# Moving normalisations, value evictions and rotary additions between the engines of a pipelined decoder layer, with new instruction lists

## The reference, cut to what matters

```python
# 1: rotary self attention, 16 heads of 16
q = (ln(x) @ Wq + bq), kv = (ln(x) @ Wkv + bkv)
q, k = rotary(q * s, x), rotary(k * s, x)      # the rotation is scaled by |x| of the row
w = softmax(causal(ln_head(q) @ ln_head(k).T / 4))
x1 = ln(x + (w @ v) @ Wo + bo)
# 2: attention along the 256 features of x1, 8 heads of 8, band of 64
q, k, v = split(x1.T @ w_in.T + b_in)
o = softmax(band(q @ k.T / sqrt(8))) @ v @ w_out.T + b_out
x2 = ln(x1 + w_ct(relu(o) * ctx) + b_ct)
# 3: feed-forward with ternary weights
g, u = x2 @ wgu.T;  h = silu(g) * u;  h = h / rms(h)
out = ln(x2 + h @ w_proj.T)
```

## Time and profile before

| | |
|---|---|
| median of three executions | 1081.5 us (1079.98 to 1083.27) |
| profiled execution, its time | 1079.87 us |
| profiled execution, its span | 1078.1 us |
| busy share of the span | PE 87%, DVE 88%, ACT 68%, POOL 76% |
| granted PE clock, mean | 0.95 of 2.4 GHz |

### The profile page before, as it was taken

How to read it: one execution, slowest core, us unless ns; L and a number is a source line. 1 busy time by engine, 2 the same in 40 slices (tenths; PEclk the granted TensorE clock), 3 DMA queues, 4 the chain that set the end, 5 groups by cost and what they waited for, 6 DMA issues and landing times.

```text
span 1078.1 us, 26386 instructions
## 1 busy us (share of the span) xinstructions
PE 933.3 (87%) x10449; PEld 547.9 (51%) x10484; DVE 944.7 (88%) x1877; ACT 734.7 (68%) x1203; POOL 816.3 (76%) x1197
## 2 busy tenths in 40 slices
PE   3366688899999999999999999999999999889885
PEld 1133355455555555555555555555555555555453
DVE  3779878899999999999999999999999999988644
ACT  1344356677778777777777777777777777777754
POOL 2764468788988888888889888888888888854542
PEclk9677679899999999999999999999999999999979
DMA  7000000000000000000000000000000000000000
GB/s 230 0 21 6 12 17 17 17 17 12 22 22 23 22 12 23 23 22 22 22 15 19 23 22 22 14 21 22 23 22 22 17 17 17 18 17 17 18 5 20
DMA packets 26122, 25.06 MB, mean 23 GB/s; under 512 B 6160, under 2 KB 24976, under 8 KB 26000
## 3 DMA queue, kind: packets, MB, share of 16 engines
q1 hardware_dynamic: 24368, 20.23, 6.6%
q10 hardware_dynamic: 1632, 3.15, 0.9%
HBM read 14.19 MB, written 4.19 MB: 17 GB/s over the span
## 4 chain that ended last, share of the span: by engine, by line
DVE 47%; PE 24%; ACT 12%; POOL 8%; issue 7%; DMA 1%; SPq 1%; POOLq 0%; DVEq 0%
DVE rowmax L1265 12%; POOL prob L1013 5%; DVE hsplit L1322 4%; ACT kT L758 4%; PE ps L420 4%; DVE amax L1209 4%; PE ps L476 3%; PE ps L386 3%; ACT prob_a L764 3%; DVE prob_a L1215 2%; POOL prob L1011 2%; DVE k_rows L1251 2%; DVE q_rows L1251 2%; DVE x L1243 2%; DVE hid L1316 2%
## 5 line engine op out<-in xcount | busy, mean ns | idle before, releaser
L1265 DVE TENSOR_REDUCE rowmax<-ps 128x4 f32<-128x768 f32 x256 | 243.0, 949 | 17.9 <-PE ps L443 17.7
L986 POOL TENSOR_TENSOR hsum<-hsum,minus_half 128x8 f32<-128x8 f32 x128 | 212.4, 1674 | 28.8 <-DVE hsum L1203 28.7
L794 ACT ACTIVATE prob<-ps 128x768 f32<-128x768 f32 x256 | 207.0, 808 | 29.2 <-PE ps L465 29.2
L1011 POOL TENSOR_SCALAR_AFFINE_SELECT prob<-prob 128x256 f32<-128x256 f32 (+1 forms) x256 | 145.9, 570 | 85.2 <-ACT prob L794 85.2
L1013 POOL TENSOR_SCALAR_AFFINE_SELECT prob<-prob 128x512 f32<-128x512 f32 (+1 forms) x256 | 160.7, 628 | 0.0
L782 ACT ACTIVATE high<-ps,bx_col 128x512 f16<-128x512 f32 x128 | 92.5, 773 | 50.8 <-PE ps L420 50.8
L476 PE MATMUL ps<-prob,v_pad 128*32 128x192 f32 x2048 | 111.2, 335 | 10.5 <-POOL prob L1013 10.3
L443 PE MATMUL ps<-k_rows,q_rows 24*128 24x192 f16 x1024 | 87.8, 250 | 4.0 <-DVE rowmax L1265 3.8
L465 PE MATMUL ps<-q_rows,k_rows 26*128 26x192 f16 x1024 | 87.6, 249 | 3.7 <-DMA q_rows<-negmax 2.1
L476 PEld LDWEIGHTS ps<-prob,v_pad 128*32 128x32 f32 x2048 | 53.9, 110 | 70.8 <-issue 43.7
L420 PE MATMUL ps<-x,wx_qk 64*128 64x256 f32 x512 | 77.2, 421 | 11.9 <-DVE hid L1316 9.4
(11 more groups left out here) (146 smaller groups left out, 2302.4 us busy)
## 6 DMA issues: line engine op xcount, KB each, us to landing
v_swap<-v_own SPq DMA_DIRECT2D x64, 68.0 KB, 2.0
xin<-in_x SPq DMA_DIRECT2D x32, 128.0 KB, 2.1
enc<-in_ctx SPq DMA_DIRECT2D x32, 128.0 KB, 2.3
out<-yout SPq DMA_DIRECT2D x32, 128.0 KB, 2.0
prob<-in_w_guT ACTq DMA_DIRECT2D x4, 512.0 KB, 6.7
prob<-in_w_projT ACTq DMA_DIRECT2D x2, 512.0 KB, 12.3
q_rows<-negmax SPq DMA_DIRECT2D x64, 8.0 KB
q_rows<-in_Wkv SPq DMA_DIRECT2D x1, 512.0 KB, 11.0
```

What stands on the lines that cost most here:

```text
L794: copy(prob[:, 2 * c:2 * c + 2, :, :].rearrange("p u a b -> p u (a b)"), ps[:, STB:STB + 2, 0:2 * QW], ACT.Exp, scale=float(XD) ** -0.5).t ...
L986: last = g.tensor_tensor(hsum[:, 1, h], hsum[:, 0, h], minus_half[:, h], ALU.pow)
L1011: g.affine_select(out=lead, in_=lead, compare_op=ALU.is_ge, fill=0.0, base=BAND - 64 * kb, pattern=[[0, 4], [1, cut]], channel_multiplier=-1)
L1265: v.tensor_reduce(of_head[:, hq:hq + 2, 2 * ng:2 * ng + 2], ps[:, MXB:MXB + 2, 0:2 * QW].rearrange("p j (a b) -> p j a b", a=2), AX, ALU.m ...
```

## The change

1. The four normalisations leave DVE. `put_xn`, `put_x1`, `put_x2` and `put_yout` become ACT activations with a per-partition scale and bias; for each, DVE makes the bias, one column. The column of eps, before the first instruction of `put_xn`, is made at the end of `put_x_stats` in a buffer of three.
2. The two value evictions, `put_v` and `put_vpad`, become plain ACT copies. The biases of the values are folded once, at the start, into `bo` and into the bias of `w_out` (`turn_bias`, `carry_bias` on PE, `hold_bias`, `add_bias` on DVE).
3. The addition of the two rotated products goes from DVE to POOL.
4. The four powers over 8 columns on POOL become one over 32 columns.
5. The low part of the maximum, its DVE instruction and its DMA go; `put_st` contracts over 25 rows, not 26.
6. The two `put_h_lo` of 512 columns become one of 1024.
7. All lists are ordered anew, `LAST_LAG` is 17, PSUM banks are dealt out anew, and many waits differ.

In the diff `v.` and `dve.` are DVE, `copy` and `act.` ACT, `g.` and `pool.` POOL, `mm`, `tr` and `pe.` PE.

```diff
-            def put_xn(t):
-                v.tensor_scalar(rot[:, 2:3], rot[:, 1:2], 4 * EPS / DIM, 1e30, ALU.mult, ALU.min)
-                v.tensor_scalar(xn[:, :], xin[:, t.buf, :], mv[:, 0, 0:1], rstd[:, 0, 0:1], ALU.subtract, ALU.mult).then_inc(S["xn"], 1)
+            def put_xn_nb(t):
+                dve.wait_ge(S["x_pow"], t.at(1, 1))
+                v.scalar_tensor_tensor(nb[:, 0, :], mv[:, 0, 0:1], -1.0, rstd[:, 0, :], ALU.mult, ALU.mult).then_inc(S["xn_nb"], 1)
+            def put_xn(t):
+                act.wait_ge(S["xn_nb"], t.at(1, 1))
+                copy(xn[:, :], xin[:, t.buf, :], ACT.Identity, bias=nb[:, 0, :], scale=rstd[:, 0, :]).then_inc(S["xn"], 1)
...
+            def put_v(t): 
+                act.wait_ge(S["v_ps"], t.at(1, 1))
+                copy(v_own[:, t.buf, :, 0:AD], ps[:, MXB + 1, 0:256].rearrange("p (h d) -> p h d", d=AD), ACT.Copy).then_inc(S["v"], 1)
+            def put_vpad(t):
+                act.wait_ge(S["vproj_ps"], t.at(1, 1))
+                copy(v_pad[:, t.buf, :, :, 0:XD], ps[:, G7, 0:DIM].rearrange("p (b u d) -> p b u d", b=2, d=XD), ACT.Copy).then_inc(S["vpad"], 1)
...
-                chain(v.tensor_tensor(rot2[:, :], rot1[:, :], rot2[:, :], ALU.add))
+                pool.wait_ge(S["rotated_c"], t.at(1, 1))
+                g.tensor_tensor(rot2[:, :], rot1[:, :], rot2[:, :], ALU.add).then_inc(S["rotated"], 1)
...
-                h = slice(8 * c, 8 * c + 8)
-                last = g.tensor_tensor(hsum[:, 1, h], hsum[:, 0, h], minus_half[:, h], ALU.pow)
+                g.tensor_tensor(hsum[:, 1, :], hsum[:, 0, :], minus_half[:, :], ALU.pow).then_inc(S["head_pow3"], 1)
...
-                sp.wait_ge(S["max_lo"], t.at(1, 1))
-                for part in range(2):
-                    sp.dma_start(q_rows[24 + part:128:32, t.buf, :, :], negmax[:, part, :]).then_inc(s_maxrow[t.buf], 16)
+                sp.wait_ge(S["max_hi"], t.at(1, 1))
+                sp.dma_start(q_rows[24:128:32, t.buf, :, :], negmax[:, 0, :]).then_inc(s_maxrow[t.buf], 16)
...
             def put_vswap(t):
+                sp.wait_ge(S["v"], t.at(1, 1))
...
-                v.scalar_tensor_tensor(hsplit[:, 1, h], hid[:, h], hss[:, 3:4], hsplit[:, 0, h], ALU.mult, ALU.subtract)
+                v.scalar_tensor_tensor(hsplit[:, 1, :], hid[:, :], hss[:, 3:4], hsplit[:, 0, :], ALU.mult, ALU.subtract).then_inc(S["h_lo1"], 1)
...
+            def turn_bias():
+                pe.wait_ge(s_fold, 1)
+                for i in range(2):
+                    last = tr(ps[:, OTB, 128 * i:128 * i + 128], qkv_bias[:, 512 + 128 * i:640 + 128 * i], ident[:, :])
+            def carry_bias():
+                pe.wait_ge(s_late, 16 * LATE)
+                pe.wait_ge(s_fold, 2)
+                for i in range(2):
+                    mm(ps[:, OTB, 256:512], zr[:, 128 * i:128 * i + 128], wo[:, i, :], start=i == 0, stop=i == 1)
+                mm(ps[:, OTB, 0:1], wx_out[:, :], bx_col[:, 12:13], start=True, stop=True).then_inc(s_turn, 1)
```

The banks: 0 and 1 (`MXB`), before only for `put_mx`, now also take in bank 0 `gate_ps0` and the second transposition of h, in bank 1 the transposition of xn, the values (`v_ps`) and the down projection, and in both the projections 1 and 3 of the second attention. A few of the waits that come with this:

```diff
             def put_xnT_ps(t):
                 pe.wait_ge(S["xn"], t.at(1, 1))
+                if t.has(4):
+                    pe.wait_ge(S["max"], t.back(4).at(8, 6))
...
             def put_down_ps(t):
+                if t.has(-6):
+                    pe.wait_ge(S["max"], t.back(-6).at(8, 7))
+                pe.wait_ge(S["hT0"], t.at(1, 1))
+                if t.has(1):
+                    pe.wait_ge(S["y3"], t.back(1).at(1, 1))
```

More of the change, by code:

```diff
@@ L31 @@
 WCHUNKS = 6
-GAINS, CONSTS, LATE = 3, 7, 9
+GAINS, CONSTS, LATE = 3, 7, 8
 class Tile:
@@ L271, in step @@
             def step(at):
-                t = at(-4)
+                t = at(-8)
                 if t:
[L274 to L281, removed]
+                    put_maxrow(t)
+                t = at(-17)
                 if t:
@@ L285, in step @@
                 if t:
-                    put_maxrow(t)
+                    put_vswap(t)
+                t = at(-2)
+                if t:
+                    put_xload(t)
+                t = at(-8)
+                if t:
+                    put_enc(t)
             steps(step)
@@ L775, in put_aT, with put_x1 @@
                 copy(attnT[:, :, :].rearrange("p a b -> p (a b)"), ps[:, G6, 0:256], ACT.Copy).then_inc(S["aT"], 1)
+            def put_x1(t):
+                act.wait_ge(S["x1_nb"], t.at(1, 1))
+                if t.has(4):
+                    act.wait_ge(S["y2"], t.back(4).at(1, 1))
+                copy(x1[:, t.x1_buf, :], y1[:, :], ACT.Identity, bias=nb[:, 1, :], scale=rstd[:, 1, :]).then_inc(S["x1"], 1)
             def put_high(t, c):
@@ L841, in put_hT, with put_yout @@
                     act.wait_ge(S["hT_ps1"], t.at(1, 1))
-                copy(hT[:, c, :, :].rearrange("p a b -> p (a b)"), bank16((G5, G7)[c]), ACT.Copy).then_inc(S[f"hT{c}"], 1)
-            def step(at):
+                copy(hT[:, c, :, :].rearrange("p a b -> p (a b)"), bank16((G5, MXB)[c]), ACT.Copy).then_inc(S[f"hT{c}"], 1)
+            def put_yout(t):
+                act.wait_ge(S["yout_nb"], t.at(1, 1))
+                if t.has(3):
+                    act.wait_ge(s_out[t.back(3).buf], t.back(3).dma(1))
+                copy(yout[:, t.buf, :], y3[:, :], ACT.Identity, bias=nb[:, 3, :], scale=rstd[:, 3, :]).then_inc(S["yout"], 1)
@@ L966, in put_x_pow @@
                 pool.wait_ge(S["x_stats"], t.at(1, 1))
+                if t.has(1):
+                    pool.wait_ge(S["xn"], t.back(1).at(1, 1))
                 g.tensor_scalar(base[:, 0, :], mv[:, 0, 1:2], EPS, None, ALU.add).then_inc(S["eps0"], 1)
@@ L1166, in put_x_stats @@
                 dve.wait_ge(s_x[t.buf], t.dma(1))
-                chain = Chain("x_stats_c", t, 3)
+                if t.has(1):
+                    dve.wait_ge(S["xn_nb"], t.back(1).at(1, 1))
+                chain = Chain("x_stats_c", t, 4)
                 chain(v.bn_stats(stat[:, 0, 0:6], xin[:, t.buf, :]))
@@ L1311, in put_hid @@
                     dve.wait_ge(S["up_ps0"], t.at(1, 1))
-                    dve.wait_ge(S["silu0"], t.at(1, 1))
+                    if t.has(1):
+                        dve.wait_ge(S["h_lo1"], t.back(1).at(1, 1))
                 if c == 1:
@@ new lines, in step @@
+                t = at(-5)
+                if t:
+                    put_x1_nb(t)
+                t = at(-4)
+                if t:
+                    put_s_sub(t)
+                t = at(-10)
+                if t:
+                    put_silu(t, 0)
+                t = at(-13)
+                if t:
+                    put_yout_nb(t)
+                t = at(-9)
+                if t:
+                    put_y2(t)
+                t = at(-6)
+                if t:
+                    put_max(t, 6)
```

1043 lines of the change are left out of this document (513 added, 530 removed).

## The result

The changed kernel takes 1008.75 us in the median of four executions (1007.86 to 1010.74), the kernel before, run beside it, 1081.97 us: a ratio of 0.933 with a 95% interval of 0.931 to 0.935. It is faster by 73 us. The forecast was 1025 us in a range of 996 to 1070. The profiled execution took 1008.2 us, with a span of 1006.2 us.

What follows compares the result with a forecast made beforehand. DVE was taken to bound full steps, with PE half a microsecond behind. Loading 18.8 + start 2 + 36.3 periods x 27.6 = 1022.7 us of span, plus 1.8 outside: 1024.5, say 1025 us, range 996 to 1070.

Steps and rivals of the forecast that it cites:

- The period: Time per full step: from 29.56 us to 27.6, with bounds of 26.4 and 28.8.
- the middle: Period of 27.6 us, between DVE's 25.1 + 1.28 = 26.4 and PE's 27.73 + about 1.1 = 28.8.
- DVE: DVE's busy time a step: loses 4.17 us, gets 1.02 back, net -3.15, from 28.29 to 25.1 us.
- ACT: ACT's busy time a step: four normalisations and two evictions add 3.0 us, from 22.29 to at most 25.3.
- this costs nothing by itself: ACT's added 3.0 us a step was to be free, since ACT had 7 us to spare.
- POOL: POOL's busy time a step: 25.38 - 6.70 + 5.40 + 1.30 = 25.4 us, unchanged; bounds 21.0 to 26.7.
- this relief: POOL instructions locked out less by DVE: some 0.5 us stretches won back, none put into the sum.
- The depth: Filling and draining: a tile's way grows by 2.3 steps, costing 0.5 periods (nothing to 1.2), 36.3 in all.
- the 215 named as its sign: Draining about 215 us long, with fewer full steps, would show the greater depth; it was 189.9 before.
- The start: Extra transpositions and products ahead of PE's first tile: some 2 us more.
- The ring: Rival: PSUM banks 0 and 1 become the bound, slower once hand-overs wait 0.3 us each; 1137 us at 0.35; chance 0.12.
- The reason: The 3.15 us a step taken off DVE come off the engine that sets the period, none hidden.

Runs made afterwards that it cites:

- a_pe_less: Changed kernel with half of the down projection's products on PE left out: 1001.03 us, ratio 0.926 to the kernel before.
- a_all_less: Changed kernel with some 0.9 us of work a tile left out on each of PE, DVE, ACT and POOL at once: 984.79 us, ratio 0.911.
- a_add_dve: Changed kernel with the addition of the rotated products back on DVE: 1027.97 us, ratio 0.951 to the kernel before.
- a_norms_dve: Changed kernel with the four normalisations back on DVE and a fifth buffer of x1: 1022.58 us, ratio 0.945 to the kernel before.
- b_norms: Kernel before with only the four normalisations moved to ACT, and the waits this needs: 1088.18 us, ratio 1.006.
- b_pow: Kernel before with only the four powers made one, at the place of the second pair; addition left on DVE: 1111.58 us, ratio 1.028.
- a_pow4: Changed kernel with the one power over 32 columns cut into four over 8, at the same place: 1038.80 us, ratio 0.960.
- b_all: Kernel before, old lists and banks, with norms and evictions on ACT, addition and one power on POOL, no low part of the maximum: 1125.69 us, ratio 1.040.

## Why the prediction was right, and where it was off

*The period* was to be 27.6 in bounds of 26.4 to 28.8 and is 27.17. 0.43 x 36.3 = 15.6 us: that is nearly all of the miss of 1025 against 1008.75. The step that was off in size is the one that took the middle between DVE with its present idle time and PE with its full busy time. The run shows PE idle for 0.51 us of a step, not for 1.1, and its busy time 26.66, in the lower half of the 26 to 27.7 given. What holds the period is neither engine's work but three loops within 0.1 us of each other, which the sum didn't look for; that a middle between two bounds came so near is in part luck.

*DVE* was to fall to 25.1 us a step: 25.17. The sum was right by errors that cancel. The columns for the normalisations were to cost 0.254 each; three cost 0.15 to 0.30 and one 0.636, together 1.26 and not 1.02. The two `put_h_lo` made one were to save some hundredths: the one takes 1.305 us where the two took 2 x 0.912, so they save 0.52, the one term of this sum that was clearly mis-sized. By rows DVE thus loses 3.43 us and not 3.15; its busy time fell by 3.12, since its instructions overlap less: its rows add up to 88.6 us more than its busy time before, and to 67.9 after.

*ACT* was to be at most 25.3: 24.39. A normalisation takes 0.59 to 0.61 us, not 0.56, an eviction 0.384 as forecast; the overlap was larger than the tenths allowed. But "this costs nothing by itself" didn't hold: by a_pe_less and a_all_less a stretch of ACT's list with three of the moved instructions is part of a loop within 0.1 us of the period.

*POOL* was to stay at 25.4: 24.20. The power of 32 columns was put at 5.40 and takes 5.48, the addition at 1.30 and takes 1.295. What was left out is, for the larger part, how long the masks take. They take 276.6 us in all; in the kernel before it was 306.6 us (94.9 + 92.6 + 65.8 + 53.3 in the same view), 0.94 us a tile more. The prediction named this relief as the lock's and put none of it into the sum. a_add_dve shows one half of it: one two-input DVE addition brings 0.48 us back. By the rule in the Trainium skill, "SBUF — State Buffer", section "Who interferes with whom", that is what such an instruction does to POOL; both traces agree. The four normalisations, which the prediction counted beside the addition, have next to no part in it: with them back on DVE (a_norms_dve) the masks take 277.0 us, and with them gone from the kernel before (b_norms) 304.9. The other half wasn't taken apart. Timing alone can bring part of it: b_pow takes nothing off DVE, and its masks take 296.7, 0.31 us a tile less than before. And POOL's time was not free: by a_pow4 its loop stands within 0.1 us of the period, so without the relief the period could have been up to 0.9 us longer. That is an estimate from these two runs; it wasn't tried.

*The depth*: 36.3 periods forecast, 36.33 measured, in part by luck, since the half period was a choice between nothing and 1.2. The draining grew by 0.83 of a period, to 196.9 us and not to the 215 named as its sign, and the filling with its further tile shrank by 0.38. *The start* was to cost 2 us more. PE's first tile does begin 2.2 us later (L338 at 23.84, before L321 at 21.64), but the first statistics of x begin at 19.0, against 18.83. So the delay lies inside the filling, which is counted in periods, and the 2 us of the sum came on top of it.

*The ring* of banks 0 and 1 didn't make the kernel slower. A maximum now waits 40.1/256 = 0.16 us for its scores, where it waited 0.07; the rival needed more than 0.3. That is the maxima's side only; the waits of the other tenants weren't summed.

*The reason* was only half right, and this matters more than the 16 us. The prediction said of the 3.15 us taken off DVE that all of it comes off the period and none is hidden. For the kernel before, with its lists, b_norms refutes that: 1.0 us less, and nothing gained. b_all takes 2.2 us off and loses 4%. In the chain before DVE had 47%, but the loop that set the period passed over POOL and ACT as well, and each of these edits lengthened it elsewhere: by the chains, POOL then waits for ACT, or the power is one long block ahead of masks and a small DVE instruction is held up beside a POOL product. The gain is made by the new lists, lags and banks together with the division of work. Undone one at a time there, the norms are worth 13 us, the addition (0.951 - 0.933) x 1082 = 19.5 and the one power (0.960 - 0.933) x 1082 = 29, 62 us of 73; undone one at a time they may count a common part twice. The power has opposite signs: -29 us in the new lists, +31 in the old, though the two edits aren't the same: in the new lists four powers at one place become one, in the old ones two of the four are moved as well. The value evictions, the low part of the maximum and the one `h_lo` weren't tried by themselves in the new lists, nor were the new lists with the old division as a whole; what each of those is worth stays open.

The Trainium skill's rule to do adds and multiplies on VectorE ("ScalarE: Activation LUTs", "Rules for kernel authors") was weighed and not followed. In the new lists ACT's norms gain 13 us although they save no work: the four take 2.40 us on ACT, as much as on DVE in a_norms_dve (0.41 to 0.77 each), and DVE's columns come on top. In the old lists they lose 6. The rule describes the instruction, and here its place in the lists decides.

## What to carry to other kernels

Ask of an edit which loop from step to step it shortens, and by how much, not only which engine it unloads: here one power on POOL for four was worth 29 us in one order of the lists and cost 31 in the other. When a pipeline is balanced, taking 0.9 us off any one engine gives nothing and putting 0.6 to 1.1 us on one costs half of it to all of it, so a cut has to be tried together with the others and with the order of the lists. One chain of waits shows only the longest loop; a lightened and a loaded variant of each engine show how near the others are, and the chain of the lightened one names the loop that is next.

## What the runs showed that was not expected

A DVE instruction on one column, L1313, takes 0.636 us where its likes take 0.15 to 0.30. The timelines of POOL and DVE at that place:

```profile
527.47 0.73 POOL L1093 TENSOR_TENSOR gated<-zr,enc 128x256 f32<-128x256 f32 x1
```
```profile
527.53 0.68 DVE L1313 SCALAR_TENSOR_TENSOR nb<-mv,rstd 128x1 f32<-128x1 f32 x1
```

It begins 0.06 us after a POOL instruction with two inputs and ends with it, to 0.01 us. So the lock works in this direction too, and costs most, as a share, on the smallest instructions. L1313 stands on the loop of POOL and DVE, and L1161 of b_pow, held up for 1.1 us, on that kernel's; whether moving such an instruction by a place would give the time back wasn't tried. In a_pow4, at the same place of DVE's list (L1316), it again takes 0.68 us.

The price of a power on POOL goes nearly with the columns: 0.587 us for one, 1.674 for eight, 5.48 for 32, and 4.5 for the 26 of a_all_less. Four times eight take 6.63 us in a_pow4, 1.15 more than one of 32: that goes with the three further instructions.
